# Attention over 2048 short sequences on one core: the value matmuls in 64x64 array tiles at another place of the step, probabilities in two buffers, and the rounding of x on ScalarE

## The chip, the cores and the metric

The kernel runs on one core of a Trainium2 chip. A core has five engines that run side by side and wait for each other through semaphores: TensorE (PE in the profile, with its weight loads in a row of their own, PEld), VectorE (DVE), ScalarE (ACT), GpSimd (POOL) and SyncE (SP), which here issues the transfers to and from HBM. The metric is the device time of one execution in microseconds (us).

## The reference, cut to what matters

```python
B, F, E = (2048, 64, 128)          # sequences, positions, features
ATT_D, HEADS = (32, 4)
q = split_heads(einsum('bfe,ed->bfd', x, W_query))     # (head, b, f, 32)
k = split_heads(einsum('bfe,ed->bfd', x, W_key))
v = split_heads(einsum('bfe,ed->bfd', x, W_value))
scores = einsum('hbqd,hbkd->hbqk', q, k)
attn = softmax(scores, axis=-1)
out = einsum('hbqk,hbkd->hbqd', attn, v)
out = out.transpose(1, 2, 0, 3).reshape(2048, 64, 128)
return relu(out + einsum('bfe,ed->bfd', x, W_res))
```

Everything is float32. x and the result have 64 MiB each.

## The kernel before

The work is cut into N = 256 steps of eight sequences (512 tokens, four tiles of two sequences, TILES = 4, SEQS = 2). Each engine runs one list of instructions, written out by hand, in which step i holds work of several neighbouring steps; TensorE's list is a loop over four steps, the others are unrolled. Only semaphores tie the lists together.

The inputs of the four projections are split in two parts that TensorE multiplies at its fast rate: x_hi is x rounded, x_lo the rest, and the weights likewise. A projection is three matmuls that add up in one PSUM bank (`w_hi*x_hi`, `w_lo*x_hi`, `w_hi*x_lo`). The scores, the transposes and the values are plain float32 matmuls. The trace shows two weight loads and two matmuls for each call of a score or value matmul, and one of each for a transpose.

TensorE's step i does, in this order:

- `weigh_values(i-2)`, L238, the value matmuls: out = probabilities x values. A pair of heads stands on the 128 rows of the array (64 keys each), so a call takes 128 rows, 64 columns (the queries of one of the two sequences) and 66 moving columns from `v_diag`, which holds the values of the two heads in a block-diagonal form. Each 33rd column is one, so that the softmax's sum comes along. 16 calls, 32 matmuls in the trace.
- `score(i)`, L217: 32 calls on tiles of 32 rows and 64 columns of the array, 64 matmuls in the trace.
- `transpose_shifted(i-1, 0)`, L229, four 128x128 transposes of the shifted scores.
- `project_qk(i+1, 0)`, L193 to L195 (queries), `project_vr(i, 0)`, L206 to L208 (values and residual of half of the tokens, six matmuls), `transpose_shifted(i-1, 1)`, `project_qk(i+1, 1)` (keys), `project_vr(i, 1)`.

The scores and the outputs of the value matmuls share the four PSUM banks of `ps_so`. So TensorE waits, before `weigh_values`, until VectorE has read the scores of the step before (`shifted_ready`) and the outputs before these (`attn_ready`).

VectorE's step i: `row_max` of the scores (L357), `shifted` = scores minus maximum (L362), the reciprocal of the sums (L368) and `attn` (L372) for step i-2, then `split_x(i+2)`: transpose of x (L342), `x_hi` (L346), `x_lo` (L348). ScalarE: relu on y (L297), exp of the transposed scores into `probs_t` (L304, twice), copies of the projections out of PSUM (L284, L291, twice each). GpSimd: y = attn + residual (L154, two instructions), then four copies that spread the values into `v_diag` (L167). SyncE: four loads of x and one store of y a step.

Of the kernel before, what the change touches and what calls it, by code (L numbers as in the profile page):

```python
# [11 lines left out]
P = 128  # L12
# [16 lines left out]
def attention_program(nc, x, w_query, w_key, w_value, w_res, out):  # L29
# [10 lines left out]
    with ExitStack() as ctx:  # L40
# [27 lines left out]
        v_diag = [sb(f"v_diag{n}", [P, SEQS, 2, HALF, PAIRS, 2, VW]) for n in range(2)]  # L68
        row_max = sb("row_max", [P, HEADS * TILES])
        shifted = [sb(f"shifted{n}", [P, TILES, HEADS, F]) for n in range(2)]  # L70
        probs_t = sb("probs_t", [P, 2, HALF * PAIRS, P])
        inv_sum = sb("inv_sum", [P, TILES, HEADS])
        attn = sb("attn", [P, 2, TILES, HEADS, D])
# [9 lines left out]
        ones_ready, diag_zero = sem("ones_ready"), sem("diag_zero")  # L83
# [63 lines left out]
        def _(pool):  # L147
            def step(i, n):
                if has(i - 2):
# [3 lines left out]
                    for a in range(2):  # L153
                        nc.gpsimd.tensor_tensor(  # L154
                            y[:, n % 2, a * HALF:(a + 1) * HALF].rearrange("k t (p j d) -> k j (t p) d", j=2, d=D),
                            attn[:, n % 2, a * HALF:(a + 1) * HALF].rearrange("k t (p j) d -> k j (t p) d", j=2),
                            vr[(n + 2) % RING][:, a, 2:4, :, :, 0:D].rearrange("k j t p d -> k j (t p) d"),
                            ALU.add).then_inc(sum_ready, 1)
                if has(i):
                    pool.wait_ge(vr_ready, halves(i, 1))  # L160
                    if has(i - 2):
                        pool.wait_ge(o_done, i - 1)
                    if has(i - 2):
                        pool.wait_ge(sum_ready, halves(i - 2, 1))
                    for j in range(2):
                        for m, seq in enumerate((1 - j, j)):
                            nc.gpsimd.tensor_copy(  # L167
                                v_diag[n % 2][j * F:(j + 1) * F, seq, :, :, :, j].rearrange("k a t p d -> k a (t p) d"),
                                vr[n][seq * F:(seq + 1) * F, :, j].rearrange("k a t p d -> k a (t p) d"),
                            ).then_inc(v_moved, 1)  # L170
                            if m == 0 or j == 1:
                                pool.wait_ge(v_moved, i * 4 + j * 2 + m + 1)
# [5 lines left out]
            for n in range(2):  # L178
                last = nc.gpsimd.memset(v_diag[n][:, :, :, :, :, :, :], 0.0)
            last.then_inc(diag_zero, 1)  # L180
            pool.wait_ge(diag_zero, 1)
# [6 lines left out]
        def _(pe):  # L188
            def project_qk(i, n, m):
                pe.wait_ge(xlo_ready, i + 1)  # L190
                if m == 1 or has(i - 1):
                    pe.wait_ge(qk_ready, halves(i, m) - 1)
                nc.tensor.matmul(ps_qk[:, :], w_hi[:, m, :], x_hi[n][:, :], start=True, stop=False)  # L193
                nc.tensor.matmul(ps_qk[:, :], w_lo[:, m, :], x_hi[n][:, :], start=False, stop=False)  # L194
                nc.tensor.matmul(ps_qk[:, :], w_hi[:, m, :], x_lo[n][:, :], start=False,  # L195
                                 stop=True).then_inc(qk_done, 1)

# [46 lines left out]
            def step(i, n):  # L244
                if has(i - 1):
                    pe.wait_ge(shifted_ready, i)
                elif not has(i):
                    pe.wait_ge(shifted_ready, N)
                if has(i - 3):
                    pe.wait_ge(attn_ready, i - 2)  # L250
# [12 lines left out]
                if has(i):  # L263
                    project_vr(i, n, 0)
                if has(i - 1):
                    transpose_shifted(i - 1, n + 1, 1)
                if has(i + 1):
                    project_qk(i + 1, (n + 1) % RING, 1)
# [139 lines left out]
```

## Time and profile before

| | |
|---|---|
| time of three runs | 1503.87, 1503.88, 1504.69 us, median 1503.88 us |
| the profiled execution: its own time, its span | 1503.88 us, 1502.1 us |
| busy: PE, PEld, DVE, ACT, POOL | 99%, 89%, 93%, 70%, 58% |
| mean granted clock of TensorE | 0.999 |

The span is what the trace covers; 1.8 us of the time lie around it. A matmul's duration in the trace runs from its start to its last result, so that neighbouring matmuls overlap and the sum of their durations exceeds the time they take; the pace is read from the distance of their starts.

### The profile page before, as it was taken

What the parts mean: (1) busy time and instruction counts of PE and PEld (TensorE: products, weight loads), DVE (VectorE), ACT (ScalarE), POOL (GpSimd) and SP (SyncE); (2) the same over time, 40 slices, a digit from 0 to 9 for tenths busy, and PEclk for the clock granted to TensorE, in tenths of its full rate; (3) what the DMA queues carried; (4) which work ended last, traced back from release to release, by engine and by line L of the source; (5) the groups of instructions that cost most, each with busy time, mean ns of one, the idle gap of its engine ahead of it and who ended that gap; (6) DMA issues with size and microseconds to landing.
All of it is one profiled execution on the core that took longest, in us unless ns stands there. A gap on an engine that the chain in (4) does not pass through costs nothing.

```text
span 1502.1 us, 73982 instructions
## 1 busy us (share of the span) xinstructions
PE 1483.0 (99%) x31232; PEld 1340.6 (89%) x31232; DVE 1390.9 (93%) x1793; ACT 1045.8 (70%) x1794; POOL 871.2 (58%) x1548
## 2 busy tenths in 40 slices
PE   7999999999999999999999999999999999999997
PEld 5999999999999999999999999999999999999996
DVE  6999999999999999999999999999999999999996
ACT  4677777777777777777777777777777777777775
POOL 3655555555555555555555555555555555555555
PEclk9999999999999999999999999999999999999999
DMA  3444444444444444444444444444444444444442
GB/s 58 99 85 97 86 97 86 97 86 96 86 97 86 97 86 96 86 96 86 97 86 96 86 96 86 96 87 96 87 96 86 96 87 96 87 95 87 95 87 76
DMA packets 677301, 135.35 MB, mean 90 GB/s; under 512 B 545888, under 2 KB 677216, under 8 KB 677216
## 3 DMA queue, kind: packets, MB, share of 16 engines
q1 hardware_dynamic: 675840, 134.30, 43.1%
q14 instruction: 74, 0.61, 0.1%
q10 hardware_dynamic: 1376, 0.26, 0.1%
q8 instruction: 11, 0.18, 0.0%
HBM read 67.37 MB, written 67.11 MB: 90 GB/s over the span
## 4 chain that ended last, share of the span: by engine, by line
PE 98%; issue 0%; POOL 0%; DVE 0%; ACTq 0%; ACT 0%; DMA 0%; POOLq 0%
PE ps_so L238 18%; PE ps_pt L229 17%; PE ps_so L217 14%; PE ps_vr L206 8%; PE ps_qk L193 8%; PE ps_qk L195 8%; PE ps_vr L208 8%; PE ps_qk L194 8%; PE ps_vr L207 8%; POOL y L154 0%; DMA w_raw<-in_L_rec_W_res_dram 0%; ACTq L327 0%; POOL v_diag L167 0%; ACT qk L284 0%; DVE row_max L357 0%
## 5 line engine op out<-in xcount | busy, mean ns | idle before, releaser
L154 POOL TENSOR_TENSOR y<-attn,vr 128x256 f32<-128x256 f32 x512 | 386.1, 775 | 523.8 <-DVE attn L372 500.2
L167 POOL COPY v_diag<-vr 64x264 f32<-64x264 f32 x1024 | 478.9, 468 | 102.9 <-POOL y L154 39.9
L304 ACT ACTIVATE probs_t<-ps_pt 128x512 f32<-128x512 f32 x512 | 307.4, 600 | 172.1 <-PE ps_pt L229 172.1
L357 DVE TENSOR_REDUCE row_max<-ps_so 128x16 f32<-128x1024 f32 x256 | 313.5, 1225 | 59.8 <-PE ps_so L217 59.5
L291 ACT COPY vr<-ps_vr 128x512 f32<-128x512 f32 x512 | 300.2, 586 | 62.0 <-PE ps_vr L208 1.4
L284 ACT COPY qk<-ps_qk 128x512 f32<-128x512 f32 x512 | 301.5, 589 | 48.8 <-PE ps_qk L195 9.2
L229 PE MATMUL ps_pt<-ident,shifted 128*128 128x128 f32 x2048 | 321.4, 279 | 0.8 <-ACT probs_t L304 0.8
L362 DVE TENSOR_TENSOR shifted<-ps_so,row_max 128x1024 f32<-128x1024 f32 x256 | 313.5, 1225 | 8.8
L238 PE MATMUL ps_so<-v_diag,probs_t 128*64 128x66 f32 x8192 | 296.1, 224 | 1.5 <-ACT probs_t L304 0.9
L238 PEld LDWEIGHTS ps_so<-v_diag,probs_t 128*64 128x64 f32 x8192 | 260.6, 137 | 36.4 <-issue 1.8
L206 PE MATMUL ps_vr<-w_hi,x_hi 128*128 128x256 f32 x1024 | 288.9, 282 | 0.0
L208 PE MATMUL ps_vr<-w_hi,x_lo 128*128 128x256 f32 x1024 | 286.6, 280 | 0.0
L207 PE MATMUL ps_vr<-w_lo,x_hi 128*128 128x256 f32 x1024 | 286.0, 279 | 0.0
L297 ACT ACTIVATE y<-y 128x512 f32<-128x512 f32 x256 | 161.5, 631 | 165.8 <-POOL y L154 165.8
L348 DVE TENSOR_TENSOR x_lo<-x_t,x_hi 128x512 fp32r<-128x512 f32 x256 | 268.3, 1048 | 8.8
L193 PE MATMUL ps_qk<-x_hi,w_hi 128*128 128x512 f32 x512 | 245.8, 480 | 10.3 <-DVE x_lo L348 9.5
L229 PEld LDWEIGHTS ps_pt<-ident,shifted 128*128 128x128 f32 x2048 | 225.9, 141 | 18.5 <-ACT probs_t L304 1.2
L217 PE MATMUL ps_so<-qk 32*64 32x64 f32 x16384 | 234.3, 231 | 0.7 <-ACT qk L284 0.7
L217 PEld LDWEIGHTS ps_so<-qk 32*64 32x64 f32 x16384 | 199.0, 131 | 19.2 <-ACT qk L284 1.4
L207 PEld LDWEIGHTS ps_vr<-w_lo,x_hi 128*128 128x128 f32 x1024 | 192.6, 188 | 24.2
L206 PEld LDWEIGHTS ps_vr<-w_hi,x_hi 128*128 128x128 f32 x1024 | 192.4, 188 | 23.6 <-ACT vr L291 0.7
L195 PE MATMUL ps_qk<-x_lo,w_hi 128*128 128x512 f32 x512 | 204.0, 398 | 0.0
(20 smaller groups left out, 1235.2 us busy)
## 6 DMA issues: line engine op xcount, KB each, us to landing
x_in<-in_r_x_dram SPq DMA_DIRECT2D x1024, 64.0 KB, 2.2
out_dram<-y SPq DMA_DIRECT2D x256, 256.0 KB, 2.5
w_raw<-in_L_rec_W_query_dram ACTq DMA_DIRECT2D x1, 64.0 KB, 2.2
w_raw<-in_L_rec_W_key_dram ACTq DMA_DIRECT2D x1, 64.0 KB, 2.6
w_raw<-in_L_rec_W_value_dram ACTq DMA_DIRECT2D x2, 32.0 KB, 2.6
w_raw<-in_L_rec_W_res_dram ACTq DMA_DIRECT2D x2, 32.0 KB, 2.5
```

The costliest lines, as they stand in the source:

```text
L154: nc.gpsimd.tensor_tensor(y[:, n % 2, a * HALF:(a + 1) * HALF].rearrange("k t (p j d) -> k j (t p) d", j=2, d=D), attn[:, n % 2, a * HALF: ...
L167: nc.gpsimd.tensor_copy(v_diag[n % 2][j * F:(j + 1) * F, seq, :, :, :, j].rearrange("k a t p d -> k a (t p) d"), vr[n][seq * F:(seq + 1) * ...
L193: nc.tensor.matmul(ps_qk[:, :], w_hi[:, m, :], x_hi[n][:, :], start=True, stop=False)
L195: nc.tensor.matmul(ps_qk[:, :], w_hi[:, m, :], x_lo[n][:, :], start=False, stop=True).then_inc(qk_done, 1)
L206: nc.tensor.matmul(ps, x_hi[n][:, tok], w_vr_hi, start=True, stop=False)
L207: nc.tensor.matmul(ps, x_hi[n][:, tok], w_vr_lo, start=False, stop=False)
L208: last = nc.tensor.matmul(ps, x_lo[n][:, tok], w_vr_hi, start=False, stop=True)
L217: last = nc.tensor.matmul(ps_so[s * F:(s + 1) * F, at:at + F], qk[rows, 0, tok], qk[rows, 1, tok], start=True, stop=True)
L229: last = nc.tensor.transpose(ps_pt[:, c * P:(c + 1) * P], pair, ident[:, :])
L238: last = nc.tensor.matmul(ps_so[s * F:(s + 1) * F, at:at + 2 * VW], probs_t[:, a, t * PAIRS + p, s * F:(s + 1) * F], v_diag[n % 2][:, s, a ...
L357: nc.vector.reduce_max(row_max[:, :].rearrange("q (h u) -> q h u", h=HEADS), scores, AX_X).then_inc(max_ready, 1)
L362: nc.vector.tensor_tensor(shifted[n % 2][:, :].rearrange("q u h f -> q h u f"), scores, row_max[:, :].rearrange("q (h u) -> q h u", h=HEAD ...
```

## The change

- The value matmuls use tiles of 64 rows and 64 columns: one head and one sequence a call, 33 moving columns, 32 calls in place of 16. Four tiles (two heads, two sequences) follow one another.
- Half of these calls read the values straight from `vr`; for the other half GpSimd copies them to the other 64 partitions (`v_cross`), two copies a step in place of four. `v_diag` and its clearing at the start go.
- In TensorE's step the value matmuls stand behind `project_qk(i+1, 1)` and before `transpose_shifted(i-1, 1)`; the transposes, which stood ahead of `project_qk(i+1, 1)`, follow them. Their waits (`wait_for_values`) stand in front of the third matmul of `project_qk(i+1, 1)`.
- `probs_t` has two buffers.
- ScalarE makes `x_hi` (`round_x(i+2)`, at the start of its step) instead of VectorE; VectorE computes `x_lo(i+2)` between `shifted` and the reciprocal, and transposes x one step earlier (`transpose_x(i+3)`, at the end of its step). ScalarE's relu moves behind the second copy of the projections for queries and keys.

```diff
@@ project_qk
                 nc.tensor.matmul(ps_qk[:, :], w_lo[:, m, :], x_hi[n][:, :], start=False, stop=False)
+                if m == 1:
+                    wait_for_values(i - 1)
                 nc.tensor.matmul(ps_qk[:, :], w_hi[:, m, :], x_lo[n][:, :], start=False,
                                  stop=True).then_inc(qk_done, 1)
+
+            def wait_for_values(i):
+                if has(i):
+                    pe.wait_ge(shifted_ready, i + 1)
+                if has(i - 3):
+                    pe.wait_ge(attn_ready, i - 2)
+                if has(i - 2):
+                    pe.wait_ge(v_moved, halves(i - 2, 1))
+                    pe.wait_ge(pt_ready, halves(i - 2, 1))
@@ weigh_values
                             for s in range(SEQS):
-                                at = (a * HALF + t) * BANK + O_AT + p * 2 * VW
-                                last = nc.tensor.matmul(
-                                    ps_so[s * F:(s + 1) * F, at:at + 2 * VW],
-                                    probs_t[:, a, t * PAIRS + p, s * F:(s + 1) * F],
-                                    v_diag[n % 2][:, s, a, t, p].rearrange("k j d -> k (j d)"), start=True, stop=True)
+                                for j in range(2):
+                                    at = (j * 2 + a) * BANK + O_AT + (t * PAIRS + p) * VW
+                                    rows, queries = slice(j * F, (j + 1) * F), slice(s * F, (s + 1) * F)
+                                    if s == j:
+                                        values = vr[(n + 2) % RING][rows, a, j, t, p]
+                                    else:
+                                        values = v_cross[n % 2][rows, a, t, p]
+                                    last = nc.tensor.matmul(ps_so[queries, at:at + VW],
+                                                            probs_t[n % 2][rows, a, t * PAIRS + p, queries], values,
+                                                            start=True, stop=True)
@@ TensorE's step
-                if has(i - 1):
-                    pe.wait_ge(shifted_ready, i)
...
-                if has(i - 2):
-                    pe.wait_ge(pt_ready, halves(i - 2, 1))
-                    pe.wait_ge(v_moved, (i - 2) * 4 + 4)
-                    weigh_values(i - 2, n)
-                if has(i):
+                if has(i):
+                    if has(i - 1):
+                        pe.wait_ge(shifted_ready, i)
+                    if has(i - 3):
+                        pe.wait_ge(attn_ready, i - 2)
                     pe.wait_ge(qk_ready, halves(i, 1))
                     score(i, 0)
...
-                if has(i - 1):
-                    transpose_shifted(i - 1, n + 1, 1)
                 if has(i + 1):
                     project_qk(i + 1, (n + 1) % RING, 1)
+                else:
+                    wait_for_values(i)
+                if has(i - 2):
+                    weigh_values(i - 2, n)
+                if has(i - 1):
+                    transpose_shifted(i - 1, n + 1, 1)
                 if has(i):
                     project_vr(i, n, 1)
@@ ScalarE's step
+                if has(i + 2):
+                    round_x(i + 2, (n + 2) % RING)
-                if has(i - 3):
-                    clip(i - 3, (n + 1) % 2)
...
+                if has(i + 1):
+                    copy_qk(i + 1, 1)
+                if has(i - 3):
+                    clip(i - 3, (n + 1) % 2)
                 if has(i - 1):
-                    exp_pt(i - 1, 1)
-                if has(i + 1):
-                    copy_qk(i + 1, 1)
+                    exp_pt(i - 1, n + 1, 1)
@@ VectorE's step
                                             ALU.subtract).then_inc(shifted_ready, 1)
+                if has(i + 2):
+                    rest_of_x(i + 2, (n + 2) % RING)
...
-                if has(i + 2):
-                    split_x(i + 2, (n + 2) % RING)
+                if has(i + 3):
+                    transpose_x(i + 3, (n + 3) % RING)
```

TensorE's list of one step in the kernel before, from its first value matmul on (ps_so holds scores and outputs, ps_pt the transposes, ps_qk and ps_vr the projections):

```order
L238 MATMUL ps_so<-v_diag,probs_t 64x66 [waits pt_ready,v_moved,attn_ready,shifted_ready]
L238 MATMUL ps_so<-v_diag,probs_t 64x66 x15
L217 MATMUL ps_so<-qk 64x64 [waits qk_ready]
L217 MATMUL ps_so<-qk 64x64 x31
L229 MATMUL ps_pt<-ident,shifted 128x128 [waits pt_ready]
L229 MATMUL ps_pt<-ident,shifted 128x128 x3
```

And in the changed kernel the stretch around the value matmuls, at the end of the step:

```order
L188 MATMUL ps_qk<-x_hi,w_hi 128x512 [waits qk_ready,xlo_ready]
L189 MATMUL ps_qk<-x_hi,w_lo 128x512
L192 MATMUL ps_qk<-x_lo,w_hi 128x512 [waits v_moved,pt_ready,attn_ready,shifted_ready]
L251 MATMUL ps_so<-vr,probs_t 64x33
L251 MATMUL ps_so<-v_cross,probs_t 64x33 x2
...
L251 MATMUL ps_so<-vr,probs_t 64x33
L236 MATMUL ps_pt<-ident,shifted 128x128 [waits pt_ready]
L236 MATMUL ps_pt<-ident,shifted 128x128 x3
L213 MATMUL ps_vr<-w_hi,x_hi 128x256 [waits vr_ready]
```

The value matmuls left the place between the last projection and the scores, and stand between a projection and a transposition. The wait for `shifted_ready` moved with them: it stood at the head of the step and asked for the scores of the step before, and now stands on the third matmul of the keys' projection and asks for the scores of the same step.

VectorE's list of one step in the kernel before:

```order
L357 TENSOR_REDUCE row_max<-ps_so 128x16 [waits s_done]
L362 TENSOR_TENSOR shifted<-ps_so,row_max 128x4x4x64 [waits pt_done,max_ready]
L368 RECIPROCAL inv_sum<-ps_so 128x16 [waits o_done]
L372 TENSOR_TENSOR attn<-ps_so,inv_sum 128x512 [waits sum_ready,inv_ready]
L342 STREAM_TRANSPOSE x_t<-x_in 128x512 [waits xlo_ready,x_loaded0]
L346 CAST x_hi<-x_t 128x512 [waits vr_done,xt_done]
L348 TENSOR_TENSOR x_lo<-x_t,x_hi 128x512 [waits xhi_ready]
```

And in the changed one:

```order
L376 TENSOR_REDUCE row_max<-ps_so 128x16 [waits s_done]
L381 TENSOR_TENSOR shifted<-ps_so,row_max 128x4x4x64 [waits pt_done,max_ready]
L367 TENSOR_TENSOR x_lo<-x_t,x_hi 128x512 [waits xhi_ready]
L389 RECIPROCAL inv_sum<-ps_so 128x16 [waits o_done]
L393 TENSOR_TENSOR attn<-ps_so,inv_sum 128x512 [waits sum_ready,inv_ready]
L363 STREAM_TRANSPOSE x_t<-x_in 128x512 [waits xlo_ready,x_loaded1]
```

The cast is gone from the list, the subtraction stands between the shifted scores and the reciprocal, and the step ends with the transpose.

## Rows read from the trace of the kernel before

**Rows 1.** The page: busy time, share of the span, instructions.
```profile
PE 1483.0 (99%) x31232; PEld 1340.6 (89%) x31232; DVE 1390.9 (93%) x1793; ACT 1045.8 (70%) x1794; POOL 871.2 (58%) x1548
```
**Rows 2.** The page: the chain that ended last.
```profile
PE 98%; issue 0%; POOL 0%; DVE 0%; ACTq 0%; ACT 0%; DMA 0%; POOLq 0%
```
**Rows 3.** The timeline of one step, TensorE: start, us, engine, instruction, count.
```profile
700.15 1.16 PE L238 MATMUL ps_so<-v_diag,probs_t 128*64 128x66 f32 x32
701.23 0.91 PE L217 MATMUL ps_so<-qk 32*64 32x64 f32 x64
702.08 0.66 PE L229 MATMUL ps_pt<-ident,shifted 128*128 128x128 f32 x4
702.46 0.19 PEld L193 LDWEIGHTS ps_qk<-x_hi,w_hi 128*128 128x128 f32 x1
702.57 0.19 PEld L194 LDWEIGHTS ps_qk<-x_hi,w_lo 128*128 128x128 f32 x1
702.81 0.39 PE L194 MATMUL ps_qk<-x_hi,w_lo 128*128 128x512 f32 x1
703.04 0.40 PE L195 MATMUL ps_qk<-x_lo,w_hi 128*128 128x512 f32 x1
...
705.12 0.28 PE L206 MATMUL ps_vr<-w_hi,x_hi 128*128 128x256 f32 x1
...
705.71 0.28 PE L208 MATMUL ps_vr<-w_hi,x_lo 128*128 128x256 f32 x1
```
**Rows 4.** The timeline, VectorE in the same step.
```profile
702.19 1.23 DVE L357 TENSOR_REDUCE row_max<-ps_so 128x16 f32<-128x1024 f32 x1 [0.20 <-PE ps_so L217]
703.45 1.22 DVE L362 TENSOR_TENSOR shifted<-ps_so,row_max 128x1024 f32<-128x1024 f32 x1
704.87 0.69 DVE L372 TENSOR_TENSOR attn<-ps_so,inv_sum 128x512 f32<-128x512 f32 x1
705.48 0.70 DVE L342 STREAM_TRANSPOSE x_t<-x_in 128x512 f32<-128x512 f32 x1
```
**Rows 5.** The timeline of PEld in three narrow stretches behind 700.14.
```profile
700.15 0.14 PEld L238 LDWEIGHTS ps_so<-v_diag,probs_t 128*64 128x64 f32 x2
700.15 0.20 PEld L238 LDWEIGHTS ps_so<-v_diag,probs_t 128*64 128x64 f32 x4
700.20 0.26 PEld L238 LDWEIGHTS ps_so<-v_diag,probs_t 128*64 128x64 f32 x6
```
**Rows 6.** PEld, narrow stretches: first two loads of the transposes at 702.08.
```profile
702.08 0.14 PEld L229 LDWEIGHTS ps_pt<-ident,shifted 128*128 128x128 f32 x1
702.14 0.25 PEld L229 LDWEIGHTS ps_pt<-ident,shifted 128*128 128x128 f32 x2
```
**Rows 7.** The timeline of the first microseconds: engines that release TensorE's weight load.
```profile
8.62 0.69 DVE L348 TENSOR_TENSOR x_lo<-x_t,x_hi 128x512 fp32r<-128x512 f32 x1
9.42 0.29 PEld L193 LDWEIGHTS ps_qk<-x_hi,w_hi 128*128 128x128 f32 x1 [9.42 <-issue]
18.29 0.59 ACT L291 COPY vr<-ps_vr 128x512 f32<-128x512 f32 x1 [0.60 <-PE ps_vr L208]
18.93 0.19 PEld L206 LDWEIGHTS ps_vr<-w_hi,x_hi 128*128 128x128 f32 x1 [0.41 <-ACT vr L291]
```
**Rows 8.** The page: groups of instructions, busy us, mean ns, idle before.
```profile
L167 POOL COPY v_diag<-vr 64x264 f32<-64x264 f32 x1024 | 478.9, 468 | 102.9 <-POOL y L154 39.9
L348 DVE TENSOR_TENSOR x_lo<-x_t,x_hi 128x512 fp32r<-128x512 f32 x256 | 268.3, 1048 | 8.8
L368 DVE RECIPROCAL inv_sum<-ps_so 128x16 f32<-128x16 f32 x256 | 63.6, 248 | 4.4 <-PE ps_so L238 4.4
L346 DVE CAST x_hi<-x_t 128x512 fp32r<-128x512 f32 x256 | 117.3, 458 | 8.8
L330 ACT CAST w_hi<-w_raw 128x512 fp32r<-128x512 f32 x1 | 0.6, 617 | 0.5 <-DMA w_raw<-in_L_rec_W_res_dram 0.5
```
**Rows 9.** Busy time in one step: PE, PEld, DVE, ACT, POOL; clock; DMA.
```profile
700.15:705.92 5.77, 5.77 (x123) 5.22 (x123) 5.43 (x8) 4.08 (x7) 3.38 (x7) 1.00 0.44 92
```

More of the change, by code:

```diff
@@ L66, in attention_program @@
         vr = [sb(f"vr{n}", [P, 2, 4, HALF, PAIRS, VW]) for n in range(RING)]
-        v_diag = [sb(f"v_diag{n}", [P, SEQS, 2, HALF, PAIRS, 2, VW]) for n in range(2)]
+        v_cross = [sb(f"v_cross{n}", [P, 2, HALF, PAIRS, VW]) for n in range(2)]
         row_max = sb("row_max", [P, HEADS * TILES])
         shifted = [sb(f"shifted{n}", [P, TILES, HEADS, F]) for n in range(2)]
-        probs_t = sb("probs_t", [P, 2, HALF * PAIRS, P])
-        inv_sum = sb("inv_sum", [P, TILES, HEADS])
-        attn = sb("attn", [P, 2, TILES, HEADS, D])
+        probs_t = [sb(f"probs_t{n}", [P, 2, HALF * PAIRS, P]) for n in range(2)]
+        inv_sum = sb("inv_sum", [P, HEADS, TILES])
+        attn = sb("attn", [P, 2, 2, TILES, PAIRS, D])
         ps_so = banks("ps_so", HEADS)
@@ L155, in step @@
                             y[:, n % 2, a * HALF:(a + 1) * HALF].rearrange("k t (p j d) -> k j (t p) d", j=2, d=D),
-                            attn[:, n % 2, a * HALF:(a + 1) * HALF].rearrange("k t (p j) d -> k j (t p) d", j=2),
+                            attn[:, n % 2, :, a * HALF:(a + 1) * HALF].rearrange("k j t p d -> k j (t p) d"),
                             vr[(n + 2) % RING][:, a, 2:4, :, :, 0:D].rearrange("k j t p d -> k j (t p) d"),
@@ L165, in step @@
                     for j in range(2):
[L166 to L172, printed above, removed]
+                        nc.gpsimd.tensor_copy(
+                            v_cross[n % 2][j * F:(j + 1) * F].rearrange("k a t p d -> k a (t p) d"),
+                            vr[n][(1 - j) * F:(2 - j) * F, :, j].rearrange("k a t p d -> k a (t p) d"),
+                        ).then_inc(v_moved, 1)
+                        pool.wait_ge(v_moved, halves(i, j))
             nc.gpsimd.memset(ident[:, :], 0.0).then_inc(ident_zero, 1)
@@ L177, in _ @@
             last.then_inc(ones_ready, 1)
[L178 to L181, printed above, removed]
             pool.wait_ge(ident_zero, 1)
@@ L293, in copy_vr, with round_x @@
                     ps_vr[:, :].rearrange("k (t j p d) -> k j t p d", t=HALF, j=4, p=PAIRS)).then_inc(vr_ready, 1)
+            def round_x(i, n):
+                act.wait_ge(xt_done, i + 1)
+                if has(i - 4):
+                    act.wait_ge(vr_done, halves(i - 4, 1))
+                nc.scalar.copy(x_hi[n][:, :], x_t[:, :]).then_inc(xhi_ready, 1)
             def clip(i, n):
@@ L330, in _ @@
             nc.scalar.copy(w_hi[:, :, :], w_raw[:, :, :]).then_inc(whi_ready, 1)
+            for i in range(2):
+                round_x(i, i)
             act.wait_ge(ones_ready, 1)
@@ L342, in split_x, with rest_of_x @@
                 nc.vector.transpose(x_t[:, :], x_in[:, n % 2]).then_inc(xt_done, 1)
-                dve.wait_ge(xt_done, i + 1)
-                if has(i - 4):
-                    dve.wait_ge(vr_done, halves(i - 4, 1))
-                nc.vector.tensor_copy(x_hi[n][:, :], x_t[:, :]).then_inc(xhi_ready, 1)
+            def rest_of_x(i, n):
                 dve.wait_ge(xhi_ready, i + 1)
@@ L381, in _ @@
                                     ALU.subtract).then_inc(wlo_ready, 1)
-            split_x(0, 0)
-            split_x(1, 1)
+            for i in range(2):
+                transpose_x(i, i)
+                rest_of_x(i, i)
+            transpose_x(2, 2)
             run(step)
```

29 lines of the change are left out of this document (13 added, 16 removed).

## The prediction

> **What bounds the kernel now.** I read the page's first part, then its chain, then the timeline of one step in the steady middle. The first part has TensorE at 99% and VectorE at 93% [rows 1]: both are full, and only the next view says which of them sets the end. The chain lies on TensorE for 98% of the span [rows 2]: it runs through its list without waiting. So the time is 256 steps of TensorE's list, and a step takes 5.77 us [rows 9] (256 x 5.77 = 1477, and 25 us of start and end make the span of 1502.1).
>
> The timeline gives what each piece of the list occupies, measured from start to start [rows 3]: value matmuls 700.15 to 701.23, 1.08 us; scores to 702.08, 0.85; four transposes to 702.46, 0.38. A 512-column matmul follows another after 0.23 (702.81 to 703.04), a 256-column one after 0.118 (five distances from 705.12 to 705.71). The step ends 5.77 behind its start; the last projection's matmul stands at 705.71, so the next value matmul starts 0.21 behind it, 0.09 more than the usual distance.
>
> Two things in these rows matter for the change. First, what a step of small array tiles costs at its borders. The value matmuls need 32 loads and matmuls in 16 rounds of two (one for each sequence, side by side). The ends of the loads lie 0.06 apart from round to round (2 done after 0.14, 4 after 0.20; 6 run out 0.26 behind 700.20 [rows 5]), so 16 rounds are 0.94 us of the 1.08. The other 0.14 is the border to the scores, which also change the shape of the tiles. Entering the value matmuls costs the same: the 0.09, and 0.05 until the first load is in (the second round's load starts at 700.20, when the first has been taken over [rows 5]).
>
> Second, what limits a round. The load for the next round starts when the matmul of this round starts, and that matmul can start only when its own load is in. Load to load is 0.05 even at the beginning, when the array holds no matmul of this kind, and 0.06 in the stream. The moving columns (66) are therefore not what paces it alone: a round can't be shorter than a load of 64 columns, about 0.055.
>
> **The change, part by part.** *The value matmuls.* The calls double and the tiles go from two to four at a time, so each tile still gets 16 rounds (8 calls x 2 passes). A call has half the moving columns but the same 64 weight columns. If the load paces the round, 16 rounds x 0.055 to 0.06 are 0.88 to 0.94: nothing to speak of is won. I take 0.94. What speaks for less is the transposes' row: there 128 columns are loaded in 0.06 (702.08 to 702.14 [rows 6]), so 64 might be loaded in 0.03. The nearest row, though, is the same kind of load, and that shows 0.05; the transposes load without the split into two passes. The far end is a round of 0.03, bound by 33 columns (half of 66): 0.48 for 16 rounds. Instructions must be delivered too: the scores' 64 matmuls take 0.85 less the border, 0.70. For this case I take 0.53, between 0.48 and 0.70 and near the end that belongs to it.
>
> The Trainium skill's page "TensorEngine Tiling (Array Packing)", section Theoretical Speedup, gives up to 2x for each dimension of at most 64, thus four tiles at once; by it the pass would halve against two tiles, and the sum below would be lower by the 0.4 us of rival A. The page "TensorE: Matmul & The Clock Gate", section LDWEIGHTS, has a load cost columns / 1.2 ns whatever the rows, 53 ns here by estimate; the rows agree for the float32 loads (0.05) and disagree for the transposes (0.06 where it has 107 ns).
>
> *The borders.* Before, the small tiles stand in one block (values, scores) with three borders: into values, values to scores, out of scores. After, scores and values stand apart, and there are four. Each is 0.14 to 0.15. One more: +0.145 us a step.
>
> *The wait.* This is the largest term. `shifted_ready` was asked for at the head of a step and concerned the scores of the step before, done long ago (shifted ended at 698.9, one step before 704.67; the value matmuls start at 700.15). Now it asks for the scores of this step, in front of the third matmul of the keys' projection. From the first load of the scores, TensorE gets there after: scores 0.85, transposes 0.38, first load of a projection 0.11 (702.46 to 702.57), three distances of 0.235 for the queries, six of 0.118 for half of the values and residual, two of 0.235 for the keys: 0.85 + 0.38 + 0.11 + 0.705 + 0.705 + 0.47 = 3.22. VectorE is done with shifted at 703.45 + 1.22 = 704.67, that is 3.44 behind 701.23 [rows 3, 4]; nothing delays or hastens it, as row_max starts when the scores are there. Between a producer's end and the load that waited for it lie 0.11 (VectorE, 9.31 to 9.42) and 0.05 (ScalarE, 18.88 to 18.93) [rows 7]; I take 0.09. Then the load of the third matmul, until then hidden, stands open: 0.11. So it starts at 3.44 + 0.09 + 0.11 = 3.64 in place of 3.22: +0.42. Behind the waiting instruction on TensorE are the value matmuls, the second transposes, half of a projection and then the next scores, on which VectorE's next row_max hangs: the loop closes, and the stall comes back in each step.
>
> *The sum.* Round the loop: third matmul at 3.64; its distance with the border to the first value load 0.21 + 0.12 = 0.33; values with their border 1.08; transposes 0.38; load 0.11; five distances of 0.118 = 0.59; to the scores' load 0.21. Together 6.34 us a step, against 5.77, which is +0.57 and agrees with 0.145 + 0.42. It applies to the 254 steps that have value matmuls and scores, nearly all: +145 us. The profiled execution took 1503.88, which is the median too; the sum gives 1649 us.
>
> *VectorE.* It loses the cast, 0.46 + 0.03 of wait, from 5.43 busy [rows 8, 9], and has 6.34 to do it in. Its x_lo, 1.05, fits between shifted at 3.47 and the end of the value matmuls at 3.97 + 1.16 = 5.13; reciprocal 0.25, attn 0.69 and transpose 0.70 end at 6.80, which is 0.46 of the next step, ahead of row_max at 0.96. attn is done at 6.10 and signalled at 6.19, 0.15 before TensorE's next scores at 6.34. Cost nothing; without that cover every later signal would add to the step.
>
> *ScalarE.* It takes the cast at 0.62 (the nearest row is its cast of the weights [rows 8]), 4.08 + 0.62 = 4.7 of 6.34. It starts at about 0.65, behind the last copy of the step before, and ends at 1.25, before the first transposes are ready at 1.54: hidden.
>
> *GpSimd and DMA.* Two copies of 0.47 fewer, 3.38 to 2.4 us a step [rows 8, 9]; it was waiting anyway. y starts when attn is done, later in a longer step. Loads and stores keep their number. All hidden. The second buffer of the probabilities takes away waits that cost nothing before. The start loses the clearing of v_diag on GpSimd, under VectorE's chain to x_lo, so nothing.
>
> **The rivals.** *A: the loads don't pace the rounds.* Then values need 0.53 in place of 0.94 and the step is 5.93, +0.16 x 254 = +41: 1545 us. For it speaks the transposes' load, against it the 0.05 between the first two rounds. *B: the wait isn't felt*, because shifted is signalled early enough or a load passes the wait: then only the border is left, 5.77 + 0.145, +37: 1541 us. Against it: the 0.22 between 3.22 and 3.44 are from rows. *C, the other side: the value matmuls run as densely as four tiles allow.* The loop without them is 6.34 - 1.08 = 5.26, so it is faster than 5.77 only if values with their border take less than 0.51 us. At 0.48 + 0.14 it isn't; it needs the border to overlap too, or the next scores to be issued faster than in the 0.85 of now, for instance 0.45 + 0.7 of scores: 5.56, -53, 1450 us. No row shows a block of 64 such matmuls in under 0.85. *D: the weight loads of the third matmul pass the wait and the signal is at its fast end*, 0.11 + 0.04 + 0.05 (rounds of 0.055 x 16 against 0.94) less: 6.14, 1598 us; it is the lower end of the likeliest case, whose upper end lets half of the scores' excess (0.70 where 8 rounds of 0.06 would be 0.48) come to the 64 value matmuls as well, +0.1: 1675 us.
>
> **How the numbers follow.** The likeliest case (0.68) is 1649 us, its own range 1598 to 1675. A has 0.16, B 0.07, C 0.06; 0.03 is left for a result within 0.2% (3 us, about what a measurement of this kernel can tell from no change), a mixture of A and a fast signal. Range: down to A and B, up to nearly the upper end, 1538 to 1672. Slower 0.91, within 0.2% 0.03, faster 0.06.
>
> **What would show it.** Right: TensorE idle for about 0.4 us a step before the third matmul of the keys (L192), released by shifted (L381); the value block L251 some 0.95 to 1.1 us long with rounds of 0.055 to 0.06 in fours; VectorE under 80% busy; a step of 6.3. Wrong: a value block of 0.6 us (A); no idle time before L192 (B); another engine named in TensorE's waits.

## The result and the profile after

The changed kernel takes 1663.89 us (median of four runs, 1663.41 to 1664.50), the kernel before 1504.17 us. The ratio is 1.1062, 95% interval [1.1042, 1.1081]. The forecast said 145 us more (1649 us); 160 were measured.

From the page of the kernel after: span, busy time of each engine (share of the span, instructions), and the chain that ended last, by engine.

```profile
span 1662.7 us, 90605 instructions
PE 1634.8 (98%) x39424; PEld 1325.8 (80%) x39424; DVE 1182.8 (71%) x1537; ACT 1178.3 (71%) x2050; POOL 551.2 (33%) x1034
...
PE 98%; issue 1%; DVE 0%; ACT 0%; ACTq 0%; DMA 0%; POOL 0%; POOLq 0%
```

Read by themselves, these lines mislead. TensorE looks as full as before [rows 1, 2], because a matmul's duration counts from its issue to its last result, and so covers most of a wait in front of the next one. What has fallen is the busy share of the weight loads, from 89% to 80%, and VectorE's, from 93% to 71%. The wait is seen where the loads are listed. The timeline of the kernel after, PEld alone, in four steps: the scores' first load (L224) and the third load of the keys' projection (L192); all other loads are left out:

```profile
698.70 0.78 PEld L224 LDWEIGHTS ps_so<-qk 32*64 32x64 f32 x64 [0.20 <-issue]
702.19 0.19 PEld L192 LDWEIGHTS ps_qk<-x_lo,w_hi 128*128 128x128 f32 x1 [0.32 <-DVE shifted L381]
...
708.63 0.19 PEld L192 LDWEIGHTS ps_qk<-x_lo,w_hi 128*128 128x128 f32 x1 [0.47 <-issue]
711.49 0.78 PEld L224 LDWEIGHTS ps_so<-qk 32*64 32x64 f32 x64 [0.19 <-issue]
715.13 0.19 PEld L192 LDWEIGHTS ps_qk<-x_lo,w_hi 128*128 128x128 f32 x1 [0.47 <-issue]
717.99 0.78 PEld L224 LDWEIGHTS ps_so<-qk 32*64 32x64 f32 x64 [0.20 <-issue]
721.48 0.19 PEld L192 LDWEIGHTS ps_qk<-x_lo,w_hi 128*128 128x128 f32 x1 [0.32 <-DVE shifted L381]
724.32 0.78 PEld L224 LDWEIGHTS ps_so<-qk 32*64 32x64 f32 x64 [0.20 <-issue]
```

Every step waits at L192. In two of four steps the load comes 3.49 us behind the scores' first load (698.70 to 702.19, 717.99 to 721.48), in the other two 3.64 (711.49 to 715.13). The steps are 6.50 us (711.49 to 717.99) and 6.33 us (717.99 to 724.32) long. The same timeline, the stretch from the shifted scores to the next scores:

```profile
700.91 1.23 DVE L381 TENSOR_TENSOR shifted<-ps_so,row_max 128x1024 f32<-128x1024 f32 x1
702.06 0.68 DVE L367 TENSOR_TENSOR x_lo<-x_t,x_hi 128x512 fp32r<-128x512 f32 x1
702.62 0.13 PEld L251 LDWEIGHTS ps_so<-vr,probs_t 64*64 64x64 f32 x1 [0.24 <-issue]
...
702.79 0.14 PEld L251 LDWEIGHTS ps_so<-v_cross,probs_t 64*64 64x64 f32 x2
...
703.49 0.14 PEld L251 LDWEIGHTS ps_so<-v_cross,probs_t 64*64 64x64 f32 x2
703.68 0.42 PEld L236 LDWEIGHTS ps_pt<-ident,shifted 128*128 128x128 f32 x4
703.82 0.26 DVE L389 RECIPROCAL inv_sum<-ps_so 128x16 f32<-128x16 f32 x1 [1.08 <-PE ps_so L251]
704.11 0.69 DVE L393 TENSOR_TENSOR attn<-ps_so,inv_sum 128x512 f32<-128x512 f32 x1
...
704.98 0.78 PEld L224 LDWEIGHTS ps_so<-qk 32*64 32x64 f32 x64
```

The value block, from its first load to that of the transposes, takes 1.06 us (702.62 to 703.68), where the block of before took 1.08 [rows 3]. Twelve rounds lie between 702.79 and 703.49, 0.058 us each. VectorE now idles 1.08 us before the reciprocal. So the value matmuls take no longer than before. Of the 160 us, 99 are idle time in front of L192 (58.3 and 40.8 us in the list of waits further down); the rest lies around it, at the first load of the value matmuls and at the next scores.

### The profile page after: what moved, and what is told of

Read it like the earlier page. It is cut to its first block, busy times and chain, and to the rows that moved or that the text cites. A ratio compares the mean times of both kernels' runs of the same rounds, so it can differ in the third digit from the quotient of the medians.

```text
span 1662.7 us, 90605 instructions
## 1 busy us (share of the span) xinstructions
PE 1634.8 (98%) x39424; PEld 1325.8 (80%) x39424; DVE 1182.8 (71%) x1537; ACT 1178.3 (71%) x2050; POOL 551.2 (33%) x1034
## 4 chain that ended last, share of the span: by engine, by line
PE 98%; issue 1%; DVE 0%; ACT 0%; ACTq 0%; DMA 0%; POOL 0%; POOLq 0%
PE ps_pt L236 18%; PE ps_so L251 16%; PE ps_so L224 14%; PE ps_qk L188 11%; PE ps_qk L192 10%; PE ps_vr L213 7%; PE ps_vr L214 7%; PE ps_vr L215 7%; PE ps_qk L189 7%; DMA w_raw<-in_L_rec_W_res_dram 0%; POOL y L155 0%; ACTq L346 0%; DVE shifted L381 0%; DVE row_max L376 0%; ACT qk L294 0%
## 5 line engine op out<-in xcount | busy, mean ns | idle before, releaser
L155 POOL TENSOR_TENSOR y<-attn,vr 128x256 f32<-128x256 f32 x512 | 340.0, 685 | 1029.6 <-issue 999.0
L236 PE MATMUL ps_pt<-ident,shifted 128*128 128x128 f32 x2048 | 335.7, 286 | 0.0
L251 PEld LDWEIGHTS ps_so<-vr,probs_t 64*64 64x64 f32 x8192 | 262.2, 134 | 64.3 <-issue 61.8
L213 PE MATMUL ps_vr<-w_hi,x_hi 128*128 128x256 f32 x1024 | 309.5, 302 | 0.0
L251 PE MATMUL ps_so<-vr,probs_t 64*64 64x33 f32 x8192 | 290.8, 221 | 2.1 <-DVE shifted L381 1.3
L251 PE MATMUL ps_so<-v_cross,probs_t 64*64 64x33 f32 x8192 | 287.4, 221 | 0.0
L389 DVE RECIPROCAL inv_sum<-ps_so 128x16 f32<-128x16 f32 x256 | 66.0, 258 | 300.2 <-PE ps_so L251 300.2
L188 PE MATMUL ps_qk<-x_hi,w_hi 128*128 128x512 f32 x512 | 251.0, 490 | 11.0 <-DVE x_lo L367 9.8
L251 PEld LDWEIGHTS ps_so<-v_cross,probs_t 64*64 64x64 f32 x8192 | 258.8, 134 | 0.0
L224 PEld LDWEIGHTS ps_so<-qk 32*64 32x64 f32 x16384 | 199.0, 131 | 47.2 <-issue 36.5
L224 PE MATMUL ps_so<-qk 32*64 32x64 f32 x16384 | 233.5, 231 | 1.1 <-ACT qk L294 0.7
L192 PE MATMUL ps_qk<-x_lo,w_hi 128*128 128x512 f32 x512 | 226.6, 443 | 7.8
L167 POOL COPY v_cross<-vr 64x264 f32<-64x264 f32 x512 | 206.9, 404 | 77.8 <-POOL y L155 41.3
```

The source lines that it names most:

```text
L155: nc.gpsimd.tensor_tensor(y[:, n % 2, a * HALF:(a + 1) * HALF].rearrange("k t (p j d) -> k j (t p) d", j=2, d=D), attn[:, n % 2, :, a * HA ...
L213: nc.tensor.matmul(ps, x_hi[n][:, tok], w_vr_hi, start=True, stop=False)
L224: last = nc.tensor.matmul(ps_so[s * F:(s + 1) * F, at:at + F], qk[rows, 0, tok], qk[rows, 1, tok], start=True, stop=True)
L236: last = nc.tensor.transpose(ps_pt[:, c * P:(c + 1) * P], pair, ident[:, :])
L251: last = nc.tensor.matmul(ps_so[queries, at:at + VW], probs_t[n % 2][rows, a, t * PAIRS + p, queries], values, start=True, stop=True)
```

## The experiments

**Tiles alone, first try.** The kernel before with the value matmuls in 64x64 tiles, at their old place. In this first try TensorE's loop over four steps is written out for all 256, and the kernel before was written out too, as the base.

```diff
-            run_looped(pe, step)
+            run(step)
```

> The kernel before with TensorE's list written out for all steps in place of the loop over four, so that every wait asks for a constant. It is the base for the next kernel. All theories: TensorE's waits are met early in the kernel before, so the form of the waits costs nothing: 1504 us, within 5.

Measured: 1511.19 us, ratio 1.0045 [1.0028, 1.0062]; the loop's removal costs 7 us (1504.36 us with it), where nothing, within 5, was expected.

> The kernel before, unrolled as its base, with one part of the change alone: value matmuls in 64x64 tiles with 33 moving columns, v_cross in place of v_diag. Place, waits, single probs_t and the cast on VectorE as before. Theory (a round is paced by its weight load, so 16 rounds stay 0.94 us, and the slowdown comes from the new place): the value block stays at 1.07 to 1.09 us from its first load to that of the scores, the time is that of the base less 0 to 6 us. Rival (the tiles themselves are slow, because 128 instructions must be delivered or because of the 64-row tiles): the base plus 50 us or more. Rival A of the prediction (loads don't pace): 0.4 us a step less, the base less 100 us, or until VectorE binds.

Measured: 1719.8 us, ratio 1.1443 [1.1417, 1.1469]. This looks like the rival's price, but the timeline of PEld in this kernel shows another thing (L211 scores, L223 transposes):

```profile
704.54 0.56 PEld L211 LDWEIGHTS ps_so<-qk 32*64 32x64 f32 x38
707.18 0.33 PEld L211 LDWEIGHTS ps_so<-qk 32*64 32x64 f32 x26 [2.08 <-issue]
707.58 0.42 PEld L223 LDWEIGHTS ps_pt<-ident,shifted 128*128 128x128 f32 x4
```

In the middle of the scores nothing is issued for 2.08 us. No other engine ends such a stall, and the kernel's waits list has 90 of them at the scores, 133 us in all and up to 2.3 us each. The mean granted clock is 0.969, where the base has 0.999: for a part of the time TensorE had the lower of its two levels (1.2 in place of 2.4 GHz), so some of the 209 us over the base is clock and not idle time. The page has the instruction queue (q8) at 312 packets and 5.11 MB; the page of before has 11 packets and 0.18 MB there, that of the base, which has no such stalls, 248 packets and 4.06 MB. This points to a long list with twice the value matmuls, and not to the tiles; which of the two it was is told by the next run, with the same tiles in a loop. That the delivery of the list is what fails stays an inference.

**Tiles alone, in the loop.** The same with the loop kept. One extra full-array matmul with two columns carries the waits.

```diff
+                    nc.tensor.matmul(ps_so[:, O_AT:O_AT + 2], w_hi[:, 0, :], w_hi[:, 0, 0:2], start=True, stop=True)
                     weigh_values(i - 2, n)
```

> The kernel before with its loop, and of the change only the value matmuls in 64x64 tiles (v_cross, 33 columns) at their old place. In front of them stands one extra full-array matmul with two moving columns that carries their waits; its output is overwritten by the values. The unrolled form of this test lost its time elsewhere: TensorE stood still in front of the scores with no engine to wait for, while the instruction queue moved 5.11 MB in place of 0.61. Theory (rounds are paced by the loads, the new place costs the time): the value block 1.07 us as in the changed kernel, the extra matmul 0.03 us, a step of 5.76 to 5.80: 1500 to 1512 us. Rival (doubling the instructions starves TensorE at this place, where 256 small instructions follow one another): steps of 6 us or more, 1560 us and up.

Measured: 1514.34 us, ratio 1.0072 [1.0058, 1.0086], 2 us above the foreseen range and far from the rival. (The 0.61 MB in the expectation is another instruction queue, q14, which moves 0.61 MB in every run.) PEld, the scores' first loads of four steps:

```profile
701.38 0.78 PEld L211 LDWEIGHTS ps_so<-qk 32*64 32x64 f32 x64
707.13 0.78 PEld L211 LDWEIGHTS ps_so<-qk 32*64 32x64 f32 x64
712.93 0.78 PEld L211 LDWEIGHTS ps_so<-qk 32*64 32x64 f32 x64
718.84 0.78 PEld L211 LDWEIGHTS ps_so<-qk 32*64 32x64 f32 x64
```

Steps of 5.75, 5.80 and 5.91 us. The best of them is 0.02 shorter than the 5.77 of before, as the theory has it; the two others are longer, at the ends of the loop over four steps. In the longest, attn ends at 717.26, the trace has an instruction of its own for attn_ready (L249) at 717.30, and the extra matmul's load follows at 717.58, where 0.12 behind the load before it, 717.42, was due; such an instruction is the subject of a test below. Why the loop's edge costs the other 0.05, and nothing with the body of before, stays open. The tiles alone, with the extra matmul (0.03 us a step, as expected above), are worth between -5 and +10 us, and don't explain +160.

**Everything but the tiles.** The changed kernel with v_diag and 66 columns again.

```diff
-                                for j in range(2):
-                                    at = (j * 2 + a) * BANK + O_AT + (t * PAIRS + p) * VW
...
+                                at = (a * HALF + t) * BANK + O_AT + p * 2 * VW
+                                last = nc.tensor.matmul(
+                                    ps_so[s * F:(s + 1) * F, at:at + 2 * VW],
+                                    probs_t[n % 2][:, a, t * PAIRS + p, s * F:(s + 1) * F],
+                                    v_diag[n % 2][:, s, a, t, p].rearrange("k j d -> k (j d)"), start=True, stop=True)
```

> The changed kernel with the value matmuls as before (128 rows, 66 moving columns, v_diag, four copies on GpSimd), but at the new place with the new waits, double probs_t and the cast on ScalarE. Theory (wait and border at the new place): steps of 6.3 to 6.5 us as in the changed kernel, 0.02 longer for the rounds: 1664 to 1672 us. Rival (the tiles themselves are slow): 1504 to 1545 us.

Measured: 1686.5 us, ratio 1.1210 [1.1192, 1.1229]. The slowdown is there without the tiles; the time is 14.5 us above the foreseen range. A step in the timeline:

```profile
703.72 1.23 DVE L381 TENSOR_TENSOR shifted<-ps_so,row_max 128x1024 f32<-128x1024 f32 x1
705.16 0.19 PEld L198 LDWEIGHTS ps_qk<-x_lo,w_hi 128*128 128x128 f32 x1 [0.48 <-POOL v_diag L168]
705.59 1.02 PEld L251 LDWEIGHTS ps_so<-v_diag,probs_t 128*64 128x64 f32 x32 [0.25 <-issue]
```

The load follows the end of shifted (704.95) by 0.21 us. POOL is named, though the values it copies are two steps old; the wait is for several semaphores. 0.21 and not 0.05 is what the next test is about. Here it is so in every step, in the changed kernel in two of four. The list of waits has, for the third load:

```profile
PEld ps_qk L198 <- issue: 60.0, 124, 0.5
PEld ps_qk L198 <- POOL v_diag L168: 58.8, 124, 0.5
```

The changed kernel has 58.3 and 40.8 us there (below), 20 us less. So of the 22 us between 1686.5 and 1663.9 about 20 are this wait, and hardly anything is left for the tiles: the long steps are 6.50 us in both kernels.

**Where the other 0.16 us come from.** TensorE's list in the loop of the changed kernel, the waits of the keys' third matmul in the first, then in the third of its four steps:

```order
L202 ISA [waits attn_ready,shifted_ready]
L192 MATMUL ps_qk<-x_lo1,w_hi 128x512 [waits pt_ready,v_moved]
```

```order
L192 MATMUL ps_qk<-x_lo3,w_hi 128x512 [waits v_moved,pt_ready,attn_ready,shifted_ready]
```

In the first two of the four steps an instruction of its own waits for shifted_ready (L202; that of the second step reads alike), in the last two the matmul does. The test moves the other three waits ahead:

```diff
+                if m == 1:
+                    wait_for_values(i - 1)
                 nc.tensor.matmul(ps_qk[:, :], w_hi[:, m, :], x_hi[n][:, :], start=True, stop=False)
                 nc.tensor.matmul(ps_qk[:, :], w_lo[:, m, :], x_hi[n][:, :], start=False, stop=False)
                 if m == 1:
-                    wait_for_values(i - 1)
+                    wait_for_shifted(i - 1)
```

> The changed kernel with three of the values' waits (attn_ready, v_moved, pt_ready) in front of the first matmul of the keys; only shifted_ready stays in front of the third. Theory (in two of four steps TensorE's list has an instruction of its own that carries shifted_ready, and the next waits come only after it, 0.16 us in all): the third load stands at 3.49 in every step, a step 0.08 us shorter on average: 1640 to 1648 us. Rival (0.16 us belong to something else in these two steps): 1660 to 1668 us.

Measured: 1645.36 us, ratio 1.0939 [1.0922, 1.0956]. Its list of waits (engine, line, waited for: us in total, times, longest):

```profile
PEld ps_qk L194 <- DVE shifted L385: 60.1, 253, 0.4
```

Now all 253 waits at the third load are for shifted, where the changed kernel had 130 for it and 124 for nobody:

```profile
PEld ps_qk L192 <- issue: 58.3, 124, 0.5
PEld ps_qk L192 <- DVE shifted L381: 40.8, 130, 0.4
```

The two together were 99 us; 60 are left, and 18.5 us of time came back, the 0.16 in half of the steps. The other 20 us of idle time only moved: the keys' first load, which has the three waits now, waits 75.6 us in all (L190) where it had waited 55.9 (L188).

**The wait behind the third matmul.**

```diff
                 nc.tensor.matmul(ps_qk[:, :], w_lo[:, m, :], x_hi[n][:, :], start=False, stop=False)
-                if m == 1:
-                    wait_for_values(i - 1)
...
-                else:
-                    wait_for_values(i)
+                wait_for_values(i)
                 if has(i - 2):
+                    nc.tensor.matmul(ps_so[:, O_AT:O_AT + 2], w_hi[:, 0, :], w_hi[:, 0, 0:2], start=True, stop=True)
                     weigh_values(i - 2, n)
```

> The changed kernel with the values' four waits behind the third matmul of the keys instead of in front of it; they are carried by the same extra matmul with two columns, directly ahead of the values. Theory (the stall is the signal of the shifted scores, 3.49 us behind the first score load, plus what stands behind it before the values): the third matmul no longer waits; the first value load moves from 3.91-4.08 to 3.70-3.86, and as attn is still done in time, the step shrinks by 0.21: 6.2 us, 1610 us (1595 to 1630). Rival (the stall has another cause, such as delivery of the instructions after it): unchanged, 1660 us or more.

Measured: 1620.41 us, ratio 1.0771 [1.0755, 1.0788], within the foreseen range. A step (L190 is the keys' third load, L273 the extra matmul, L249 the values):

```profile
700.75 1.22 DVE L379 TENSOR_TENSOR shifted<-ps_so,row_max 128x1024 f32<-128x1024 f32 x1
701.75 0.19 PEld L190 LDWEIGHTS ps_qk<-x_lo,w_hi 128*128 128x128 f32 x1
702.02 0.19 PEld L273 LDWEIGHTS ps_so<-w_hi 128*128 128x128 f32 x1
702.31 0.13 PEld L249 LDWEIGHTS ps_so<-vr,probs_t 64*64 64x64 f32 x1
703.51 0.26 DVE L387 RECIPROCAL inv_sum<-ps_so 128x16 f32<-128x16 f32 x1 [0.94 <-PE ps_so L249]
703.81 0.69 DVE L391 TENSOR_TENSOR attn<-ps_so,inv_sum 128x512 f32<-128x512 f32 x1
704.73 0.78 PEld L222 LDWEIGHTS ps_so<-qk 32*64 32x64 f32 x64 [0.19 <-issue]
```

The third load no longer waits: it stands at 701.75, before shifted ends at 701.97. The extra matmul's load, which carries the waits, starts at 702.02, and the values 0.29 later. Then VectorE has its turn: attn is done at 704.50 and the scores' load follows at 704.73. So, against the expectation, attn wasn't done in time for the scores, and 0.17 us a step came back (43 us) of the expected 0.21.

**More work between the scores and the wait.** The second transposes back ahead of the keys' projection.

```diff
                 if has(i):
                     project_vr(i, n, 0)
+                if has(i - 1):
+                    transpose_shifted(i - 1, n + 1, 1)
...
                     weigh_values(i - 2, n)
-                if has(i - 1):
-                    transpose_shifted(i - 1, n + 1, 1)
```

> The changed kernel with the second transposes back ahead of the keys' projection (and ScalarE's second exp ahead of its copy), so 0.44 us more work stands between the scores and the third matmul of the keys. All else as changed. Theory (the wait for the shifted scores): the third load would be due 3.42 us behind the first score load, the signal is there at 3.49, and at 3.65 in two of four steps; the stall shrinks from 0.4-0.5 to 0.1-0.2, the border stays: a step of 6.0 to 6.15, 1565 to 1600 us. Rival (the tiles or the rounding cost the time, not the wait): unchanged, 1664 us.

Measured: 1670.4 us, ratio 1.1103 [1.1084, 1.1121]: a miss, 6 us slower than the changed kernel. A step:

```profile
694.60 0.78 PEld L224 LDWEIGHTS ps_so<-qk 32*64 32x64 f32 x64 [0.59 <-issue]
696.81 1.22 DVE L381 TENSOR_TENSOR shifted<-ps_so,row_max 128x1024 f32<-128x1024 f32 x1
698.09 0.19 PEld L192 LDWEIGHTS ps_qk<-x_lo,w_hi 128*128 128x128 f32 x1
700.07 0.69 DVE L393 TENSOR_TENSOR attn<-ps_so,inv_sum 128x512 f32<-128x512 f32 x1
701.00 0.78 PEld L224 LDWEIGHTS ps_so<-qk 32*64 32x64 f32 x64 [0.58 <-issue]
701.00 0.91 PE L224 MATMUL ps_so<-qk 32*64 32x64 f32 x64 [0.38 <-DVE attn L393]
```

In this step the third load has no idle time marked any more (698.09, still 3.49 behind 694.60); in two of four it still waits, 34.8 us in 124 times, 0.28 us each, where 0.1 to 0.2 was foreseen. But the transposes were also what stood between the values and the next scores. Without them TensorE reaches the scores before attn is done (700.76) and idles 0.58 us there. The stall has moved from shifted to attn. The expectation worked out the first wait and took the second, which had 0.15 us of slack in the prediction, as met.

**The rounding of x.** Back on VectorE.

```diff
-                if has(i + 2):
-                    round_x(i + 2, (n + 2) % RING)
...
+                nc.vector.tensor_copy(x_hi[n][:, :], x_t[:, :]).then_inc(xhi_ready, 1)
                 dve.wait_ge(xhi_ready, i + 1)
```

> The changed kernel with the rounding of x back on VectorE, directly ahead of x_lo, and gone from ScalarE. Theory: VectorE has 0.6 us of idle time before the reciprocal and 0.57 before row_max, so the cast's 0.5 us fits in the first: 1664 us, within 5. Rival (VectorE's load sets the step): 0.2 us a step or more, 1710 us; rival (the rounding on ScalarE costs time): below 1655 us.

Measured: 1663.41 us, ratio 1.1060 [1.1043, 1.1077], the same as the changed kernel. VectorE's idle time before the reciprocal took the cast in, as the theory has it; this part of the change is worth nothing, either way.

**What sets a round.** The kernel tiles_old_place with 32 query columns as weights in place of 64; the outputs of the other queries are left out. (Four full-array matmuls at the start, which write the columns of `ps_so` once, come in addition.)

```diff
-                                    rows, queries = slice(j * F, (j + 1) * F), slice(s * F, (s + 1) * F)
+                                    rows, queries = slice(j * F, (j + 1) * F), slice(s * F, s * F + BLK)
```

> The kernel tiles_old_place with value matmuls for the first 32 of the 64 queries of each sequence alone (half of the probabilities' columns are loaded as weights, half of the outputs is left out); as many matmuls, 33 moving columns as before. It tells what sets a round of 0.058 us. Theory (a weight load is paid by its columns): rounds of about 0.03, bound then by 33 moving columns or by delivery, a value block of 0.55 to 0.75 us in place of 1.07, a step 0.3 us shorter or until VectorE binds at about 5.4: 1410 to 1440 us. Rival (a load is a fixed latency of about 0.055 that the next round waits for, whatever its columns): block and time unchanged, 1510 to 1518 us.

Measured: 1440.16 us, ratio 0.9573 [0.9558, 0.9588], the upper edge of what the theory expected. Two narrow stretches of its timeline, the first value load and the scores' first load:

```profile
702.47 0.10 PEld L238 LDWEIGHTS ps_so<-vr,probs_t 64*32 64x32 f32 x1
...
703.16 0.78 PEld L211 LDWEIGHTS ps_so<-qk 32*64 32x64 f32 x64
```

The block takes 0.69 us in place of 1.07, with the same number of matmuls and the same 33 moving columns. So with 64 weight columns the load paces the round, and it is paid by its columns; and 128 instructions can be delivered well within the 1.07 us. The time of the whole kernel says less, since VectorE now binds too: the chain that ended last lies on it for 38% of the span, and on TensorE for 41%.

**A try for a faster version.** The tiles at the old place without the extra matmul; the waits stand in front of the last matmul of the projection before.

```diff
+                    if a == 1 and t == 1:
+                        wait_for_values(i + 1)
                     last = nc.tensor.matmul(ps, x_lo[n][:, tok], w_vr_hi, start=False, stop=True)
```

> The kernel tiles_old_place without its extra matmul: the values' waits stand in front of the last matmul of the step's second values-and-residual projection, 0.3 us before the values. A try for a version that beats both kernels. If the signals are early enough: 0.02 us a step less than the kernel before in the steps without a loop edge, 1499 to 1510 us. If attn_ready, which came some 0.1 us before that matmul's load in the kernel before, is late: 1515 to 1530 us.

Measured: 1534.33 us, ratio 1.0198 [1.0184, 1.0212]. Slower than tiles_old_place, and 4 us above the second expectation's range. Its four steps take 5.96, 6.02, 5.78 and 5.77 us. The end of the step of 6.02:

```profile
702.04 0.69 DVE L377 TENSOR_TENSOR attn<-ps_so,inv_sum 128x512 f32<-128x512 f32 x1
702.64 0.19 PEld L210 LDWEIGHTS ps_vr<-w_lo,x_hi 128*128 128x128 f32 x1
703.05 0.19 PEld L213 LDWEIGHTS ps_vr<-w_hi,x_lo 128*128 128x128 f32 x1 [0.22 <-issue]
```

The load at 703.05 was due at 702.76. attn ends at 702.73, so its signal is hardly late; the load follows it by 0.32 us. The trace has an instruction of its own for attn_ready (L196) at 702.77, and others for two of the other waits behind it, before the load. The step of 5.96 has 0.28 us in front of the first value load instead, with no releaser, and its cause stays open. No version here with all outputs beats the kernel before.

## Why the prediction was right

*What bounds the kernel and the value block.* Right. Rounds stay at 0.058 us with 33 moving columns, the block came out at 1.06 us against 1.08 in the sum. half_queries shows the mechanism: half the weight columns, 0.69 us. Rival A (the loads don't pace) is refuted by both. Its ground, a load of 128 columns in 0.06 us, was misread: 0.06 is the distance of the first two loads of the transposes alone. The row 702.14 of [rows 6] holds two loads of 0.14 us that end 0.25 behind its start, so the third load stands 0.11 behind the second, and the fourth again 0.11 behind the third:

```profile
702.25 0.25 PEld L229 LDWEIGHTS ps_pt<-ident,shifted 128*128 128x128 f32 x2
```

So these rows don't disagree with the 107 ns that the prediction set against them. The first distance of a block isn't a measure of the load either, neither the 0.06 here nor the 0.05 at the start of the values: it hardly changes between 128 and 64 columns. The Trainium skill's page "TensorEngine Tiling (Array Packing)", section Theoretical Speedup, gives up to 2x for each small dimension; here a second halving of the rows was worth 0.02 us of 1.08, since the columns of the load stayed at 64.

*The wait.* Right in place and mechanism, near in size. The third load was put at 3.44 + 0.09 = 3.53 us behind the scores; it stands at 3.49 in two steps and 3.64 in two. The signal itself takes 0.05 (702.14 to 702.19); what I hadn't counted is that the waits are not all carried by the matmul, which adds 0.16 in half of the steps, as waits_split shows. The mean is 3.57, +0.04 us a step.

*The border.* Consistent: the step out of the last projection into the scores is there in addition to that into the values. It wasn't tested by itself.

*The way back to the scores.* Mis-sized, and the reason for transposes_first. The sum let the scores start 0.21 us behind the last projection's matmul and held attn_ready met by 0.15 us. The end of attn itself was right, 6.10 us behind the scores (704.80 against 698.70), in the steps where the third load stands at 3.49. But in three of four steps the scores wait:

```profile
710.56 0.69 DVE L393 TENSOR_TENSOR attn<-ps_so,inv_sum 128x512 f32<-128x512 f32 x1
...
711.10 0.19 PEld L215 LDWEIGHTS ps_vr<-w_hi,x_lo 128*128 128x128 f32 x1
```

The last projection's load is issued at 711.10 and attn ends at 711.25; the scores' load at 711.49 (shown at the top) follows the one by 0.39 and the other by 0.24, where the sum had 0.09 behind attn. Here too an instruction of its own carries attn_ready, at the code's L261; the trace between 708 and 720 has two:

```profile
L261 PEldq EVENT_SEMAPHORE  x2: 51/51/51, 711.3 to 717.8; - x2
```

In the fourth step (704.98) the load follows attn by 0.18 and the last projection's load by 0.32, as in the sum. That is about 0.06 us a step above the sum on average. With +0.04 from the first wait and -0.03 from the shorter blocks the mean of the four steps is 6.41 in place of 6.34, and 0.06 to 0.07 x 254 = 15 to 18 us; 1649 and 1664 lie 15 apart. The three differences are small and partly cancel, so the nearness of the total is a little better than that of its terms.

*What was costed at nothing.* The rounding on ScalarE: right, by round_on_vector. GpSimd and the transfers: no wait of TensorE ends with them in the changed kernel. VectorE under 80% busy: 71%. One step of the cover was thinner than said: the keys' projection now waits 0.17 us for ScalarE's copy of the queries (the transposes had stood between), at L188; the time is inside the later wait for shifted and costs nothing.

*Rival B, the wait isn't felt:* refuted. Moving the wait back by one matmul gave 43 us; the scores then still followed the end of attn, by 0.23 us. *Rival C, faster:* refuted; the fastest form of the tiles tried, with all outputs, took 1514 us.

Together: before, one stretch of TensorE's list wrote both kinds of results to the shared banks, values and then scores, and VectorE's two turns on them (2.5 us and 0.97 us) lay in one stretch of other work. After, scores and values stand apart, and each step holds both turns one after the other: scores, VectorE, values, VectorE, scores. move_only shows that the slowdown is there without the tiles, round_on_vector that the rounding has no part in it; the second buffer of the probabilities wasn't tested by itself. wait_later and transposes_first show that shortening one turn's wait leaves the other's. That the two turns are forced by the shared banks is argued from the code. In each bank the scores lie in columns 0 to 255 and the outputs from 256 on, so the waits don't protect overlapping data; whether they could be dropped wasn't tried, nor a version with separate banks (the outputs need 16 x 33 = 528 columns, and the kernel's bank has 512).

## What to carry to other kernels

Before you move work in the list of a full engine, follow the loop through every engine that it hands its results to, and add it up with each moved wait in it: a wait that was met 1 us early at one place bound at the other, and shortening it brought the next. Read idle time from the weight loads, since matmul rows cover it. And before splitting small matmuls into more tiles ask what paces a tile's round; if it is the load, only fewer weight columns help.

## What the runs showed of the hardware

- The same value rounds took 0.058 us with 66 and with 33 moving columns and 64 weight columns; with 32 weight columns the block fell from 1.07 to 0.69 us. The loads of the transposes, 128 columns wide, stood 0.06 us apart at first and 0.11 from then on.
- A wait carried by the load that needs it is followed in 0.05 us; with an instruction of its own between, it took 0.21 us.
- TensorE's list written out for 256 steps cost 7 us in the kernel before, and in the kernel with 64x64 tiles brought stalls of up to 2.3 us with no releaser and a mean granted clock of 0.969. The loop over four had neither: no wait in front of the scores in its middle, and 0.998.
- x_lo on VectorE took 1048 ns [rows 8], overlapping GpSimd's additions and copies, and 682 ns in the changed kernel, where GpSimd is idle at that time, with the same shapes. In tiles_old_place, where it overlaps them again, it took 1049. No run changes the overlap alone.
